# Values by slots, and position terms with keys on the partitions, turned by an identity product

## The chip, the cores and the metric

The kernel runs on one core of a Trainium2 chip. Its time is the device time of one execution in microseconds (us); the number to predict is the median of the runs. TensorE is called PE here, ScalarE ACT, VectorE DVE, GpSimd POOL, and SP is the engine that issues nearly all DMAs.

## What is computed

A decoder layer in float32 on x of 4 x 256 x 128 and a context of 4 x 512 x 128: local attention, cross attention, and a mixture of 12 experts. The change touches the first part alone:

```python
q_blocked = pad(q).reshape(B, nb, 12, 8, 16)          # 22 blocks of 12 queries, 8 heads of 16
k_ctx = _extract_block_context(k, nb)                 # 24 keys for each block: 12 past, 12 own
v_ctx = _extract_block_context(v, nb)
matrix_ac = einsum('bnchd,bnkhd->bhnck', q_blocked, k_ctx)
rel_k = (position_embeddings @ Wrel.T).reshape(-1, H, D)      # 25 positions
matrix_bd = _rel_shift(einsum('bnchd,phd->bhncp', q_blocked, rel_k))
logits = tanh((matrix_ac + matrix_bd) / 50) * 50
out = einsum('bhnck,bnkhd->bnchd', softmax(logits), v_ctx)
```

`_rel_shift` gives row c (query c of its block) the position term of key j at position j - c, with a wrap by one row: where j < c, the term is that of query c-1 at position j - c + 25.

## The kernel before, in words

Each engine has one program, written out by hand in the order in which it runs; semaphores join them. The 88 windows (4 batches x 22 blocks) are taken four at a time, 32 PSUM partitions each: 22 groups, in 6 chunks `c` of at most 4 groups. `qM` holds the queries of a window in 24 columns (12 for each half of the heads), `kM` the keys times a mask of four heads (`G` = 4), so that one product of 96 columns gives a window's logits for 24 keys and 4 heads. `relM` is the same for the 25 positions (100 columns).

PE, after the projections (`L863`): `relative(c)` multiplies every window's queries with `relM`; ACT copies the results to `bd_raw` (`positions_out`, `L631`), SP stores them in DRAM (`store_positions`, `L382`) and reads them back with rows one element further on each time (`shift_positions`, `L392`) into `bd`: that is the shift. `local_logits(c)` (`L922`) makes the key terms in PSUM, DVE adds `bd` (`add_positions`, `L1383`), ACT does tanh and exp in place (`local_softmax`, `L673`, `L675`), PE turns the result (`turn_weights_local`, `L931`), ACT copies it to `prT` (`weights_turned`, `L682`), and PE multiplies with the values (`local_values`, `L953`). DVE divides (`local_normalize`, `L1405`, `L1407`), PE turns (`turn_outputs`, `L966`) and projects (`local_project`, `L975`).

The values of a window must lie with 96 partitions = 24 keys x 4 heads in `vbd`, zero outside their own head. They go PSUM, `v_tok` (ACT `L638`), DRAM (`v_dram`, `L399`), `vbd` (24 DMAs, `spread_values`, `L351`, behind all the position traffic on SP).

Between the logits and the turned weights stand eight products of the cross attention, `unit(0)` to `unit(7)` (`L892`): four key units, each read by DVE (`key_unit`, `L1357`, `L1362`) with POOL adding the halves (`L506`), and four value units, read by ACT (`value_unit`, `L665`). They share two PSUM banks in turn, so that each waits for the reader of the one before the last. `local_values(0)` uses these banks as well. DVE's order after the key units: the first three `add_positions`, the statistics of contexts 1 to 3 (`L1294`), three more `add_positions`, their normalisation (`L1300`), then `local_normalize(0)`.

Of the kernel before, what the change touches and what calls it, by code (L numbers as in the profile page):

```python
# [7 lines left out]
P = 128  # L8
BANK = 512
F32 = mybir.dt.float32  # L10
F32R = mybir.dt.float32r
ALU = mybir.AluOpType
# [11 lines left out]
def decoder_layer(nc, x, ctx_in, pos, a_wq, a_wk, a_wv, a_wpost, a_wrel, a_pds,  # L24
# [31 lines left out]
    REL = NPOS * G  # L56
    SPREADS = 3
# [42 lines left out]
    with ExitStack() as ctx:  # L100
# [6 lines left out]
        bd_dram = nc.dram_tensor("bd_dram", [WALL, QW, REL], F32, kind="Internal").ap()  # L107
        gate_dram = nc.dram_tensor("gate_dram", [2, NE, 4 * P], F32, kind="Internal").ap()
        v_dram = nc.dram_tensor("v_dram", [B * SPAD, VROW], F32, kind="Internal").ap()
        psum = ctx.enter_context(nc.psum_tensor("psum", [P, 8, BANK], F32))  # L110

        REL_BANK = [3, 1, 7, 6, 0, 2]
# [16 lines left out]

        def half_groups(half):  # L130

            return slice(CG * HCH * half, min(CG * HCH * (half + 1), NGRP))
# [5 lines left out]
        def bank(i, parts=P):  # L138
# [45 lines left out]
        v_tok = sb("v_tok", [P, NT, HA, DE], F32, first)  # L184
        v_pad = sb("v_pad", [PAST, HA, DE], F32, first)
# [7 lines left out]
        relM = sb("relM", [P, NPOS, G], F32, first)  # L193
        vbd = sb("vbd", [GK, NW, G, 2, DE], F32, first)
        projected = ExitStack()
        xT = sb("xT", [P, B, S], F32, projected)

        bd_raw = sb("bd_raw", [P, NGRP, REL], F32, projected)
# [5 lines left out]
        first.close()  # L204

# [56 lines left out]
            ld_affine ld_wo ld_bo bd_stored0 bd_stored1 shifted0 shifted1 stored consts chain_pool chain_dve chain_act stats_done mv_done  # L262
            rstd_done xn_done absneg_done softplus_done qscale_done awT_ps awT_done xT_ps xT_done v_tok_ps v_tok_done pad_set v_zeroed v_padded v_stored v_spread0 v_spread1 v_spread2
            rel_ps relM_done q_ps k_ps qM_done kM_done bd_ps bd_raw_done added_done pT_ps pT_done logit_ps
# [72 lines left out]
        def _(sp):  # L337
# [7 lines left out]
            def spread_values(third):  # L345

                ns = spread_slots(third)
                windows = v_dram.rearrange("(n t) c -> t n c", t=CH)
                for g in range(G):
                    for part in range(2):  # L350
                        sp.dma_start(vbd[part * CH * G + g:(part + 1) * CH * G:G, ns, g, :, :].rearrange("t n h d -> t n (h d)"),  # L351
                                     windows[:, ns.start + part:ns.stop + part, g * 2 * DE:(g + 1) * 2 * DE]).then_inc(s[f"v_spread{third}"], 16)
# [13 lines left out]
            sp.wait_ge(s["pad_set"], 2)  # L366
            rows = v_dram.rearrange("(b r) c -> r b c", b=B)
# [1319 lines left out]
```

## Time and profile before

| | us |
|---|---|
| median of 3 runs | 478.07 |
| lowest, highest | 477.93, 480.35 |
| the profiled execution, whole | 479.27 |
| its span (first to last instruction) | 477.5 |
| PE busy, share of the span | 92% |
| DVE, POOL, ACT busy | 69%, 51%, 40% |

The rows come from the one profiled execution. A row of the chain of waits is a piece of the path that ended last; a row of the timeline is one or several instructions of an engine with their first start and their length. float32 products are two instructions each, so a row with x16 holds 8 products. PE's granted clock is 1.00 at 2.4 GHz and 0.50 at 1.2 GHz.

### The profile page before, as it was taken

What the parts mean: (1) busy time and instruction counts of PE and PEld (TensorE: products, weight loads), DVE (VectorE), ACT (ScalarE), POOL (GpSimd) and SP (SyncE); (2) the same over time, 40 slices, a digit from 0 to 9 for tenths busy, and PEclk for the clock granted to TensorE, in tenths of its full rate; (3) what the DMA queues carried; (4) which work ended last, traced back from release to release, by engine and by line L of the source; (5) the groups of instructions that cost most, each with busy time, mean ns of one, the idle gap of its engine ahead of it and who ended that gap; (6) DMA issues with size and microseconds to landing.
All of it is one profiled execution on the core that took longest, in us unless ns stands there. A gap on an engine that the chain in (4) does not pass through costs nothing.

```text
span 477.5 us, 8551 instructions
## 1 busy us (share of the span) xinstructions
PE 441.5 (92%) x3264; PEld 325.0 (68%) x3264; DVE 327.2 (69%) x688; ACT 188.7 (40%) x296; POOL 245.4 (51%) x217
## 2 busy tenths in 40 slices
PE   4977899999999999989999998779999999999996
PEld 2654676766666766657766675367777688888885
DVE  8886578979998577895779767635463543274544
ACT  7738046456445354553444543213344532300000
POOL 5783139896898768877677766114232333000000
PEclk9997799999999999999999999588999999999999
DMA  7754400000000000000000030230325140000000
GB/s 182 185 126 66 79 14 2 0 1 1 0 1 2 1 1 1 0 1 2 1 1 2 1 93 0 80 121 28 128 68 198 67 155 1 1 12 5 12 5 11
DMA packets 32810, 19.83 MB, mean 42 GB/s; under 512 B 16438, under 2 KB 29675, under 8 KB 32771
## 3 DMA queue, kind: packets, MB, share of 16 engines
q1 hardware_dynamic: 32068, 19.02, 14.6%
q8 instruction: 26, 0.43, 0.4%
q10 hardware_dynamic: 702, 0.28, 0.2%
q14 instruction: 14, 0.11, 0.1%
HBM read 17.27 MB, written 2.02 MB: 40 GB/s over the span
## 4 chain that ended last, share of the span: by engine, by line
PE 75%; DVE 14%; ACT 5%; issue 4%; POOL 2%; DVEq 0%; POOLq 0%; ACTq 0%
PE psum L1083 11%; PE psum L1066 9%; PE psum L892 9%; PE psum L1257 5%; PE psum L1256 5%; PE psum L1258 5%; PE psum L1220 4%; PE psum L1222 4%; PE psum L1221 4%; PE psum L1102 3%; PE psum L1093 3%; PE psum L995 2%; PE psum L1119 2%; DVE kM L1369 2%; PE psum L953 2%
## 5 line engine op out<-in xcount | busy, mean ns | idle before, releaser
L514 POOL TENSOR_TENSOR e_part<-e_sb 128x512 f32<-128x512 f32 x64 | 88.6, 1401 | 30.7 <-DVE e_sb L1467 30.7
L744 ACT ACTIVATE e_sb<-psum 128x1024 f32<-128x1024 f32 x64 | 62.2, 1022 | 17.0 <-PE psum L1066 16.8
L1083 PE MATMUL psum<-e_sb,v_sb 128*64 128x256 f32 x512 | 64.3, 394 | 0.0
L1066 PE MATMUL psum<-q_t,kT 64*128 64x256 f32 x512 | 64.3, 389 | 0.0
L545 POOL TENSOR_TENSOR xeT_lo<-xeT,xeT_hi 128x512 fp32r<-128x512 f32 x24 | 30.9, 1288 | 58.9 <-ACT xeT_hi L758 50.0
L1467 DVE TENSOR_SCALAR e_sb<-e_sb 128x1024 f32<-128x1024 f32 x64 | 56.2, 913 | 5.4 <-ACT e_sb L744 5.4
L1474 DVE RECIPROCAL rden<-psum 128x256 f32<-128x256 f32 x32 | 55.9, 1746 | 3.7 <-PE psum L1093 3.6
L1651 DVE SCALAR_TENSOR_TENSOR x_sb<-psum,dw,x_sb 128x128 f32<-128x128 f32 x96 | 33.6, 350 | 34.8 <-PE psum L1258 32.2
L1066 PEld LDWEIGHTS psum<-q_t,kT 64*128 64x128 f32 x512 | 47.0, 186 | 10.3 <-issue 5.4
L724 ACT ACTIVATE kT<-psum 128x512 f32<-128x512 f32 x32 | 19.1, 598 | 86.4 <-PE psum L995 86.4
L506 POOL TENSOR_TENSOR k_rot<-rope_a,rope_b 128x512 f32<-128x512 f32 x32 | 42.2, 1321 | 18.7 <-DVE rope_b L1362 18.7
L1083 PEld LDWEIGHTS psum<-e_sb,v_sb 128*64 128x64 f32 x512 | 34.4, 139 | 22.4 <-issue 6.9
L1220 PE MATMUL psum<-xeT_hi,w1T_hi 128*128 128x512 f32 x96 | 41.1, 428 | 3.4 <-POOL xeT_lo L545 3.4
L520 POOL TENSOR_TENSOR e_part<-e_part 128x512 f32<-128x512 f32 x32 | 41.5, 1296 | 2.5
L1221 PE MATMUL psum<-xeT_lo,w1T_hi 128*128 128x512 f32 x96 | 38.7, 403 | 0.0
L1222 PE MATMUL psum<-xeT_hi,w1T_lo 128*128 128x512 f32 x96 | 38.7, 403 | 0.0
L758 ACT ACTIVATE xeT_hi<-xeT 128x512 fp32r<-128x512 f32 x24 | 15.1, 632 | 58.9 <-DVE xeT L1506 36.1
L1256 PE MATMUL psum<-w2T_hi,h_hi 128*128 128x512 f32 x96 | 37.3, 389 | 0.0
L1257 PE MATMUL psum<-w2T_lo,h_hi 128*128 128x512 f32 x96 | 37.3, 389 | 0.0
L1258 PE MATMUL psum<-w2T_hi,h_lo 128*128 128x512 f32 x96 | 37.3, 389 | 0.0
L892 PE MATMUL psum<-wkv_hi,ctx_hi 128*128 128x512 f32 x64 | 31.5, 492 | 5.7 <-DVE rope_b L1362 5.7
L1357 DVE TENSOR_TENSOR rope_a<-psum,cos_sb 128x512 f32<-128x512 f32 x32 | 22.0, 686 | 20.3 <-PE psum L892 19.9
(191 smaller groups left out, 786.5 us busy)
## 6 DMA issues: line engine op xcount, KB each, us to landing
w_raw<-in_L_ffn_W_dram SPq DMA_DIRECT2D x24, 256.0 KB, 2.8
gates<-gate_dram SPq DMA_DIRECT2D x6, 768.0 KB, 4.4
ctx_sb<-in_ctx_dram SPq DMA_DIRECT2D x4, 256.0 KB, 6.1
vbd<-v_dram SPq DMA_DIRECT2D x16, 52.6 KB
v_dram<-v_tok SPq DMA_DIRECT2D x4, 136.0 KB, 3.1
raw<-in_L_xattn_Wkv_dram SPq DMA_DIRECT2D x2, 256.0 KB, 4.9
k_rot<-in_L_xattn_Wkv_dram SPq DMA_DIRECT2D x2, 256.0 KB, 4.9
k_rot<-in_L_xattn_Wq_dram SPq DMA_DIRECT2D x2, 256.0 KB, 5.4
```

Source lines behind the costliest of these rows:

```text
L514: pool.tensor_tensor(e_part[:, p % 2, half, :, :], e_sb[:, i % ERING, :, 0, :], e_sb[:, i % ERING, :, 1, :], ALU.add)\
L744: act.activation(e_sb[:, i % ERING, :, :, :].rearrange("p a k t -> p (a k t)"), psum[:, a:a + 2, :].rearrange("p a b -> p (a b)"), ACT.Exp ...
L892: mm = pe.matmul(o, c, w_[:, wc:wc + GC], start=(part == 0), stop=(part == 2))
L1066: mm = pe.matmul(psum[:, 2 * (i % 2) + a, t * S:(t + 1) * S], kT[rows, p % 3, kt * P:(kt + 1) * P], q_t[rows, j % 2, p % 2, :], start=True ...
L1083: mm = pe.matmul(psum[DX * a:DX * a + DX, pv_bank(p), 0:S], v_sb[g % 2][:, kt, 2 * pp + a, :], e_sb[:, i % ERING, a, t, :], start=(kt == 0 ...
L1220: pe.matmul(bank(c), w1T_hi[:, e, c, :], hi, start=(e == 0), stop=False)
L1221: pe.matmul(bank(c), w1T_hi[:, e, c, :], lo, start=False, stop=False)
L1222: mm = pe.matmul(bank(c), w1T_lo[:, e, c, :], hi, start=False, stop=(e == NE - 1))
L1256: pe.matmul(o, hi, w_hi, start=(c == 0), stop=False)
L1257: pe.matmul(o, hi, w_lo, start=False, stop=False)
L1258: mm = pe.matmul(o, lo, w_hi, start=False, stop=(c == HC - 1))
L1467: dve.tensor_scalar(e, e, E_LO, E_HI, ALU.max, ALU.min).then_inc(s["clip_done"], 1)
```

## The change

**Values.** `v_tok` gets one row for each of 96 slots (a slot is 12 padded tokens; 23 for each batch, 92 in all). 12 products (one for each token of a slot, the slot's columns of `xT` at a stride of 12) take the place of 8. `xT` gets its zero padding in SBUF, so the padding rows in DRAM go. `v_dram` is ordered token, head group, slot, so that each of the 24 spreading DMAs moves 12 long pieces instead of 12 x 33 short ones; the 3 stores before them have 96 x 16 pieces of 136 bytes each.

**Position terms.** `relative(j)` now has the positions as stationary operand: for query c of all 88 windows, the 96 columns of `relM` that begin at c positions less give keys on the partitions and windows on the columns, and a second product with the columns 25 positions on adds the wrap. 46 products of 64 rows x 96, 88 columns each; the two halves of the heads lie on the two halves of the rows. ACT copies them to `rel_t` (6 copies, 96 x 352). `local_logits` adds them in PSUM by a second product for each window, `rel_t` times the identity, 88 in all. The DRAM tensor `bd_dram`, its 8 stores and 16 loads, the 6 additions on DVE and the clearing of `bd` on POOL are gone.

**Order.** PE makes the values first, then the positions, then logits and turned weights in alternation, and only then units 1 to 7. ACT does the softmax before the value units. DVE makes all of `kM` before it normalises context 0.

```diff
-            def positions_out(c):
-                act.wait_ge(s["bd_ps"], c + 1)
-                ks = groups(c)
-                act.activation(bd_raw[:, ks.start:ks.stop, :].rearrange("p k r -> p (k r)"), psum[:, REL_BANK[c], 0:len(ks) * REL], ACT.Copy)\
-                   .then_inc(s["bd_raw_done"], 1)
+            def positions_out(n):
+                j, h = divmod(n, 2)
+                act.wait_ge(s["rel_t_ps"], j + 1)
+                q = h * CH + CPB * j
+                act.activation(rel_t[:, 0:WALL * QW].rearrange("p (w q) -> p q w", q=QW)[:, q:q + CPB, :],
+                               psum[0:GK, REL_BANK[n], 0:CPB * WALL].rearrange("p (c w) -> p c w", c=CPB), ACT.Copy).then_inc(s["rel_t_done"], 1)
...
-                act.wait_ge(s["added_done"], c + 1)
+                act.wait_ge(s["logit_ps"], c + 1)
...
-                act.activation(at, at, ACT.Tanh, scale=1.0 / CAP).then_inc(s["capped_done"], 1)
+                act.activation(at, psum[:, LOGIT_BANK[c], 0:len(ks) * GK], ACT.Tanh, scale=1.0 / CAP).then_inc(s["capped_done"], 1)
...
             def weights_turned(c):
                 act.wait_ge(s["pT_ps"], c + 1)
                 if c == 0:
-                    act.wait_ge(s["bd_stored1"], 16 * WG)
+                    act.wait_ge(s["v_stored"], 16 * len(VBANK))
...
+            def relative(j):
+                if j == 0:
+                    pe.wait_ge(s["relM_done"], G)
+                    pe.wait_ge(s["rel_set"], 2)
+                    pe.wait_ge(s["qM_done"], 8)
+                else:
+                    pe.wait_ge(s["v_tok_done"], 1 if j == 1 else 3)
+                queries_at = qM[:, 0:WALL * QW].rearrange("p (w q) -> p q w", q=QW)
+                for cc in range(CPB):
+                    c = CPB * j + cc
+                    main = slice(REL_AT - G * c, REL_AT - G * c + GK)
+                    wrap = slice(REL_AT + REL - G * c, REL_AT + REL - G * c + GK)
+                    for part in range(2 if c else 1):
+                        for h in range(2):
+                            rows = slice(64 * h, 64 * h + 64)
+                            mm = pe.matmul(psum[0:GK, REL_BANK[2 * j + h], cc * WALL:(cc + 1) * WALL], relM[rows, wrap if part else main],
+                                           queries_at[rows, h * CH + c - part, :], start=(part == 0), stop=(part == 1 or c == 0))
+                mm.then_inc(s["rel_t_ps"], 1)
...
+            def local_logits(c):
+                pe.wait_ge(s["kM_done"], G if c == 0 else 2 * G)
+                pe.wait_ge(s["rel_t_done"], len(REL_BANK))
...
+                        pe.matmul(psum[QT * i:QT * i + QT, LOGIT_BANK[c], at:at + GK], qM[:, QW * w:QW * w + QT],
+                                  kM[:, b, CH * n:CH * n + CTX, :].rearrange("p t g -> p (t g)"), start=True, stop=False)
+                    for i in range(WG):
+                        w = WG * k + i
+                        mm = pe.matmul(psum[QT * i:QT * i + QT, LOGIT_BANK[c], at:at + GK], rel_t[:, QW * w:QW * w + QT],
+                                       ident[0:GK, 0:GK], start=False, stop=True)
...
-            for c in range(HCH):
-                relative(c)
             values = awT[:, 2, :].rearrange("p (h g d) -> p g h d", h=2, g=G)
-            for t in range(NT):
...
+            for t in range(CH):
+                j, at = divmod(t, VT)
+                mm = pe.matmul(psum[0:SLOTS, VBANK[j], at * D:(at + 1) * D].rearrange("p (g h d) -> p g h d", g=G, h=2),
+                               xT[:, t:SLOTS * CH:CH], values, start=True, stop=True)
...
+            for j in range(CH // CPB):
+                relative(j)
             for c in range(NCH):
                 local_logits(c)
-            for m in range(UNITS):
+                if c == 1:
+                    turn_context(0, 6, "ct_ps")
+                if c >= 2:
+                    turn_weights_local(c - 2)
+            turn_weights_local(NCH - 2)
+            unit(0)
+            turn_weights_local(NCH - 1)
+            for m in range(1, UNITS):
                 unit(m)
-            for c in range(NCH):
-                turn_weights_local(c)
```

PE from the projections on, before: products by line, output<-operands, shape and count.

```order
L863 MATMUL psum<-xT,awT 128x512 x4
L908 MATMUL psum<-relM,qM 32x100 x48
L1018 MATMUL psum<-awT,xT 128x128 x8
L908 MATMUL psum<-relM,qM 32x100 x40
L870 MATMUL psum<-ident,ctx_sb 128x128 x4
L922 MATMUL psum<-kM,qM 32x96 x88
```

The same place after the change (`L1003` are the values, `L888` the positions, `L907` the identity products; the last two rows repeat to the end of each chunk).

```order
L839 MATMUL psum<-xT,awT 128x512 x4
L1003 MATMUL psum<-awT,xT 96x128 x12
L888 MATMUL psum<-qM,relM 96x88 x46
L903 MATMUL psum<-kM,qM 32x96 x4
L907 MATMUL psum<-ident,rel_t 32x96 x4
```

What moved: the 88 position products of 32 rows became 46 of 96 rows behind the values, and every four key products are followed by four identity products.

ACT from the position copies to the first copy of turned weights, before.

```order
L631 ACTIVATE bd_raw<-psum 128x400 x2
L631 ACTIVATE bd_raw<-psum 128x200
L647 ACTIVATE ctx_f<-psum,affine 128x512
L653 ACTIVATE ctx_hi<-ctx_f 128x512
L595 ACTIVATE wkv_hi<-k_rot 128x512 x2
L597 ACTIVATE wq_hi<-k_rot 128x512 x2
L691 ACT_TABLE_LOAD
L665 ACTIVATE v_sb<-psum 128x512 x4
L673 ACTIVATE bd<-bd 128x384
L675 ACTIVATE bd<-bd 128x384
```

The same stretch after the change.

```order
L612 ACTIVATE v_tok<-psum 96x32x16 x3
L607 ACTIVATE rel_t<-psum 96x4x88 x6
L569 ACTIVATE wkv_hi<-k_rot 128x512 x2
L571 ACTIVATE wq_hi<-k_rot 128x512 x2
L665 ACT_TABLE_LOAD
L645 ACTIVATE bd<-psum 128x384
L647 ACTIVATE bd<-bd 128x384
L621 ACTIVATE ctx_f<-psum,affine 128x512
L627 ACTIVATE ctx_hi<-ctx_f 128x512
L645 ACTIVATE bd<-psum 128x384
```

What moved: the context's copies (`L647`, `L653` before) went behind the first softmax, and the four value units (`L665` before) behind all of it.

## Rows read from the trace of the kernel before

**Rows 1.** Page, part 2: granted clock of PE in 40 slices of the span.

```profile
PEclk9997799999999999999999999588999999999999
```

**Rows 2.** The chain that ended last, in order of time: start us, length us, what.

```profile
25.39 3.18 PE psum L922 x144
28.57 0.91 PE psum L892 x3
...
37.71 0.60 ACT v_sb L665
...
46.43 3.80 PE psum L953 x128
50.24 1.03 PE psum L966 x4
...
52.44 0.60 PE psum L966 x4
...
58.51 1.99 PE psum L953 x64
...
79.54 1.93 PE psum L1066 x16
```

**Rows 3.** Timeline of PE: start, length, line, shapes [idle before].

```profile
16.07 2.27 PE L908 MATMUL psum<-relM,qM 128*32 128x100 f32 x96
18.27 2.05 PE L1018 MATMUL psum<-awT,xT 128*128 128x128 f32 x16
...
39.33 0.64 PE L931 MATMUL psum<-ident,bd 128*96 128x128 f32 x4 [1.65 <-ACT bd L675]
...
51.19 1.25 PE L953 MATMUL psum<-vbd,prT 96*32 96x68 f32 x64
```

**Rows 4.** Timeline of ACT.

```profile
17.03 0.51 ACT L631 ACTIVATE bd_raw<-psum 128x400 f32<-128x400 f32 x1
...
22.86 0.78 ACT L647 ACTIVATE ctx_f<-psum,affine 128x512 f32<-128x512 f32 x1 [0.22 <-PE psum L870]
...
24.21 1.13 ACT L595 ACTIVATE wkv_hi<-k_rot 128x512 fp32r<-128x512 f32 x2
...
26.40 1.28 ACT L691 ACT_TABLE_LOAD   x1
...
40.63 0.51 ACT L673 ACTIVATE bd<-bd 128x384 f32<-128x384 f32 x1
...
42.08 0.51 ACT L673 ACTIVATE bd<-bd 128x384 f32<-128x384 f32 x1
```

**Rows 5.** Timeline of DVE.

```profile
14.46 4.18 DVE L1369 TENSOR_SCALAR kM<-psum,mask 128x512 f32<-128x512 f32 x4 [1.97 <-PE psum L863]
...
29.57 0.69 DVE L1357 TENSOR_TENSOR rope_a<-psum,cos_sb 128x512 f32<-128x512 f32 x1 [1.62 <-PE psum L892]
...
34.92 1.48 DVE L1383 TENSOR_TENSOR bd<-psum,bd 128x384 f32<-128x384 f32 x3
36.32 0.86 DVE L1294 BATCH_NORM_STATS2 stats<-ctx_sb 128x6 f32<-128x128 f32 x4
...
41.02 3.15 DVE L1300 TENSOR_SCALAR ctx_sb<-ctx_sb,mv,rstd 128x128 f32<-128x128 f32 x12
48.52 0.36 DVE L1405 RECIPROCAL rq<-psum 128x32 f32<-128x32 f32 x1 [4.35 <-PE psum L953]
48.91 0.69 DVE L1407 TENSOR_TENSOR o_q<-psum,rq 128x512 f32<-128x512 f32 x1
```

**Rows 6.** Timeline of SP: issue of DMAs.

```profile
35.26 20.52 SPq L351 DMA_DIRECT2D vbd<-v_dram  x24
```

**Rows 7.** Page, DMA to landing of the values' stores: KB each, us to landing.

```profile
v_dram<-v_tok SPq DMA_DIRECT2D x4, 136.0 KB, 3.1
```

**Rows 8.** Stretches of 2 us: PE, PEld, DVE, ACT, POOL busy, PE's granted clock, DMA share, GB/s.

```profile
38.00:40.00 2.00, 0.64 (x4) 0.39 (x4) 1.93 (x15) 1.94 (x5) 1.92 (x3) 1.00 0.52 77
...
46.00:48.00 2.00, 2.00 (x62) 1.64 (x65) 0.00 (x0) 0.74 (x2) 0.00 (x0) 0.50 0.55 82
```

More of the change, by code:

```diff
@@ L56, in decoder_layer @@
     REL = NPOS * G
+    SLOTS = 96
+    CPB = 4
+    REL_AT = CH * G
+    VBANK = [0, 2, 3]
+    VT = CH // len(VBANK)
     SPREADS = 3
@@ L192, in decoder_layer @@
         pds = sb("pds", [P, 4], F32, first)
-        relM = sb("relM", [P, NPOS, G], F32, first)
-        vbd = sb("vbd", [GK, NW, G, 2, DE], F32, first)
+        relM = sb("relM", [P, REL_AT + REL + GK], F32, first)
+        vbd = sb("vbd", [GK, G, NW, 2, DE], F32, first)
         projected = ExitStack()
-        xT = sb("xT", [P, B, S], F32, projected)
-        bd_raw = sb("bd_raw", [P, NGRP, REL], F32, projected)
+        xT = sb("xT", [P, SLOTS * CH], F32, projected)
+        v_tok = sb("v_tok", [SLOTS, CH, G, 2, DE], F32, projected)
+        rel_t = sb("rel_t", [GK, WALL * QW + QT - QW], F32, projected)
         projected.close()
@@ L204, in decoder_layer @@
         first.close()
+        xT_b = xT[:, 0:B * SPAD].rearrange("p (b t) -> p b t", b=B)
+        vbd_all = vbd[:, :, :, :, :].rearrange("p g n h e -> p (g n h e)")
+        VZ = [G * NW * 2 * DE * i // 3 for i in range(4)]
         second = ExitStack()
@@ L526, in _ @@
                 key_sum(k)
[L527 to L528 removed]
+            pool.wait_ge(s["logit_ps"], NCH)
+            pool.wait_ge(s["v_stored"], 16 * len(VBANK))
             pitch = CG * P + CH
@@ L691, in _ @@
             act.preload_act_table(ACT.Exp)
-            for m in range(KC, UNITS):
-                value_unit(m)
             local_softmax(0)
+            act.wait_ge(s["ct_ps"], 1)
+            context_f(0)
             for c in range(1, NCH):
@@ L698, in _ @@
             weights_turned(NCH - 1)
+            for m in range(KC, UNITS):
+                value_unit(m)
             for c in range(HCH):
@@ L953, in local_values @@
                             mm = pe.matmul(psum[QT * i:QT * i + QT, o, at:at + G * DE].rearrange("p (g e) -> p g e", e=DE),
-                                           prT[:, q:q + QT], vbd[:, NBP * b + n, :, half, :], start=True, stop=True)
+                                           prT[:, q:q + QT], vbd[:, :, NBP * b + n, half, :], start=True, stop=True)
                 mm.then_inc(s["oa_ps"], 1)
@@ L1376, in _ @@
             dve.wait_ge(s["sin_done"], 1)
-            def add_positions(c):
-                dve.wait_ge(s["logit_ps"], c + 1)
-                dve.wait_ge(s[f"shifted{c // HCH}"], 16 * 2 * WG)
-                ks = groups(c)
-                dve.tensor_tensor(bd[:, ks.start:ks.stop, :].rearrange("p k r -> p (k r)"), psum[:, LOGIT_BANK[c], 0:len(ks) * GK],
-                                  bd[:, ks.start:ks.stop, :].rearrange("p k r -> p (k r)"), ALU.add).then_inc(s["added_done"], 1)
             for m in range(KC):
                 key_unit(m)
-            for c in range(HCH):
-                add_positions(c)
             for b in range(1, B):
                 context_statistics(b)
-            for c in range(HCH, NCH):
-                add_positions(c)
             for b in range(1, B):
```

137 lines of the change are left out of this document (43 added, 94 removed).

## The prediction

> **What bounds the kernel now.** I read the 40 slices first: PE's clock is full except in slices 4 and 5 (36 to 60 us) and around 300 us [rows 1]. The change acts before 66 us; from there on the chain is PE work in an unchanged order, so what counts is by how much its entry into that part moves. Next the chain of waits up to there. It goes through the last logits and the eight units (28.57 us on), then ACT's softmax after the last value unit (37.71), then the value products at 46.43, the first turned outputs at 50.24 and the second at 52.44 [rows 2]. The long idle piece is PE between 37.7 and 46.4: it waits for ACT, is busy 0.64 of 2 us, and enters the value products at 1.2 GHz [rows 8]. The position terms' trip through DRAM is not what ends last there: ACT is busy with value units until 38.3 us in any case. The spreading of the values is issued from 35.26 to 55.78 us [rows 6]; its last third is used at 58.51 [rows 2].
>
> **What the change does to each stage.** I follow four times: the end of the position products R, the end of the last copy to rel_t E, the start of unit 0 U, and the start of the second turned outputs T, which was 52.44 us [rows 2].
>
> *Values.* They start where the position products did, 16.07 us. Eight products took 2.05 us, 0.256 us each [rows 3]; twelve take 3.07 us and end at 19.14. The queries are complete at 17.03 [rows 4], so they don't bind.
>
> *Positions.* 46 products, 92 instructions of 64 rows with 96 stationary and 88 moving columns: no row has this shape. The 64-row products of the scores, whose halves lie on the two halves of the rows as here, take 1.93 us for 16 instructions with 256 moving columns [rows 2], 121 ns each; by moving columns 88/256 of that is 41 ns, by stationary columns (128 there) 96/128 of it is 90 ns. So 3.8 to 8.3 us. Before, 96 instructions of 32 columns took 2.27 us, but four of them lie side by side [rows 3]. I take the middle, 65 ns: the shape lies between the two scalings, since a narrow moving operand leaves less to hide the loading of weights behind. 6.0 us, so R = 25.1.
>
> The Trainium skill ("TensorE: Matmul & The Clock Gate", LDWEIGHTS) has the load of weights grow with its columns, at 1.2 per ns, and lets it run ahead of a product only where the row groups differ. By that 96 columns are 80 ns, 7.4 us in all if loads never lie side by side, and the result would be 481.3; no row here shows a load of 96 columns in a stream.
>
> *Copies to rel_t.* 400 columns took 0.505 us [rows 4]; 352 take about 0.46 if the spread writing costs nothing. DVE's kM copy, which writes one float32 of four, takes 1.05 us for 512 columns where its rope_a product takes 0.69 [rows 5], a factor of 1.5. So 0.46 to 0.70; I take 0.55. Four of the six hide beside the products; the last two follow R: E = 25.1 + 0.15 + 1.1 = 26.4 us.
>
> *ACT from E to U.* The four weight copies (24.21 to 26.40) and the table load of 1.28 us come behind the copies: 3.5 us [rows 4]. Then a softmax of 0.97 (tanh 0.51 and exp of the same length, overlapped), the context's two copies that moved here, 1.35 (22.86 to 24.21), three rounds of softmax and copy at 1.45 (40.63 to 42.08) and a last softmax of 0.97 [rows 4]: 7.65. PE then turns once more, 0.64 [rows 3], so U = E + 11.8. PE's own work in the same time is less: 176 logit products are 352 instructions at 22 ns (144 in 3.18 us [rows 2]), 7.8 us, twice before; five turns at 0.6 and the context's turn make 11.4. It is hidden by 0.4 us only; if the switch between key and identity products costs 30 ns instead of 22, PE is later by 2.4 us. U = 38.2 us. DVE's six additions (three in 1.48 us [rows 5]) go, but what they held up stood behind the value units anyway.
>
> *Units and values.* The eight units still alternate over two banks with DVE: 28.57 to 38.3 with the last copy, 9.8 us [rows 2]. So value products start at U + 9.85 = 48.0, where before it was 46.43. That is the cost of the change: the softmax, which stood behind the units, now stands ahead of them, and what PE gains by not waiting it spends on logits. They then run at 2.4 GHz: 128 instructions take 2.5 (64 in 1.25 [rows 3]) where they took 3.80 [rows 2]. PE is through both at 50.5.
>
> *What is late next: DVE.* Its order keeps context statistics and normalisation between the key units and the first division. The key units end 6.4 us after U (28.57 to 34.92, where the additions began). From the first statistics to the normalisation went 4.7 (36.32 to 41.02), of which the second three additions, one of half size, were 1.2 by the 1.48 of the first three; so statistics take 3.5, normalisation 3.1 [rows 5], which before ended at 44.2 with room to 48.52. Now it ends at U + 13.1 = 51.3, and the division takes 1.08 (48.52 to 49.60 [rows 5]): turned outputs start at 52.4, not 50.24. So half of the gain of the full clock goes into a wait for DVE. Then turn 0.6, values 1.2: T = U + 16.0 = 54.2 against 52.44, +1.8 us. From there the chain is the one of before.
>
> *DMA.* Three stores of 1536 pieces each take the place of four of 256. The nearest issue row is the spreading, 24 issues of up to 396 pieces in 20.52 us [rows 6], 2.2 ns a piece: 3.3 us each. They start at about 17.8, end by 27.7 and land 3.1 later [rows 7], 30.8. ACT's first turned copy needs them at E + 6.8 = 33.2. Between a price by bytes alone (0.5 us each) and this, nothing waits. The 24 spreading DMAs with 12 pieces end long before 48 us at any of these prices; their old cost was hidden, so nothing is gained.
>
> *The rest at nothing.* The clearing of bd, the padding's memsets and the small relM memsets on POOL lie ahead of work that waits for statistics. Where that cover is gone, they cost under 0.5 us.
>
> **The sum.** +1.8 us at the entry into the unchanged part. The profiled execution took 479.27, its span 477.5, the rest 1.8 around it; it lies 1.2 above the median of 478.07. By its own measure it would be 481.1, by the median **479.9 us**.
>
> **The rivals.**
> *A, the halves pair fully.* 92 instructions at 43 ns, 4.0 us, copies of 0.46: R = 23.1, E = 24.2, U = 36.0, T = 52.0, -0.4: 477.6. For it: the scores' halves do pair. Against it: there the moving part is three times as long. Chance 0.25.
>
> *B, strided reading.* The queries are read with 96 bytes between columns, the slots' weights with 48. If every column costs a second access, the halves' gain is lost: 88 ns each, 8.1 us, copies 0.70: R = 27.2, E = 28.8, U = 40.6, T + 4.2: 482.3. For it: DVE's kM row [rows 5]; against it: no PE row shows such a cost. Chance 0.15. The Trainium skill ("SBUF — State Buffer", the note on cachelines) states this: lines of 16 bytes, and at least two hits in each for full bandwidth.
>
> *C, the stores hold ACT.* The first turned copy now waits for v_stored. It decides from a store of 4.1 us on; at 5.8 each they land at 38.3, ACT stands 5.1 us, and all behind it: 485.0. For it: 136-byte pieces, 4608 of them; against it: the issue row gives 3.3. Chance 0.07.
>
> *D, the clock.* The dip in which 64 instructions take 1.99 and not 1.25 us (58.51 us [rows 2, 3]) goes, since PE no longer stands idle ahead of it: -1.3 beside A's -0.4: 476.4, and a little below with the later dip near 300 us moved. Against it: the work just ahead of 58 us is as thin as before, and there is a new gap of 1.9 us before the turned outputs. Chance 0.08.
>
> **Chances.** Forecast 0.45 (478.5 to 481.8), A 0.25, B 0.15, C 0.07, D 0.08. About 0.5%, 2.4 us, is what a measurement can tell from no change. Below 475.7 lies the end of D, 0.05; above 480.5 lie B, C and two fifths of the forecast, 0.40; within, 0.55. The range takes in A, B and most of D, with 2 us for B's upper bounds (the identity products at 30 ns): 476.2 to 484.0.
>
> **What would show it.** Position products of 6 us ending near 25; ACT's first tanh near 30; unit 0 near 38 and value products near 48 at clock 1.00; then DVE normalising contexts while PE stands until about 52.4. It would be wrong if DVE had done its contexts earlier (the gain of the clock is then real, -1.5), if the identity products run slower than 22 ns, or if PE's clock falls between 25 and 48 us.

## The result, and the profile after

The changed kernel takes 490.78 us (median of 4 runs, 489.21 to 493.47), the kernel before 478.00 in the same session: a ratio of 1.027, 95% interval 1.020 to 1.033. It is slower, and 10.9 us above the 479.9 that was predicted, outside the range. The profiled execution took 489.21, its span 487.5 against 477.5. It is the fastest of its four, and the profiled execution of before lies above its median, so the profiles show 10.0 of the 12.8 us between the medians. Some executions further below ran slower at a lower granted clock, among them the profiled one of `y_layout` (0.85 on the mean), whose rows are therefore not shown, and all ratios leave them out.

The slices first, then the timeline of PE after the change (start, length, line, shapes, idle before).

```profile
PEclk9959989999999999999999999787999999999999
```

```profile
15.94 4.90 PE L1003 MATMUL psum<-awT,xT 128*96 128x128 f32 x24
20.77 10.33 PE L888 MATMUL psum<-qM,relM 64*96 64x88 f32 x92
...
33.16 0.55 PE L903 MATMUL psum<-kM,qM 128*32 128x96 f32 x8 [2.07 <-issue]
...
37.49 0.36 PE L903 MATMUL psum<-kM,qM 128*32 128x96 f32 x8
...
56.79 2.23 PE L938 MATMUL psum<-vbd,prT 96*32 96x68 f32 x128 [0.89 <-ACT v_sb L637]
61.04 0.97 PE L951 MATMUL psum<-ident,o_q 128*128 128x128 f32 x4 [2.02 <-DVE o_q L1384]
61.94 2.06 PE L938 MATMUL psum<-vbd,prT 96*32 96x68 f32 x64
63.93 0.98 PE L951 MATMUL psum<-ident,o_q 128*128 128x128 f32 x4
...
70.12 1.25 PE L938 MATMUL psum<-vbd,prT 96*32 96x68 f32 x64
```

The second turned outputs begin at 63.93 us; before they began at 52.44 [rows 2]. So 11.5 us are lost ahead of the part that the change leaves alone, 1.5 are given back behind it (0.7 of them by the value products at 70.12, which take 1.25 us where those of before at 58.51 took 1.99 [rows 2]), and 10.0 remain in the span. The loss is all in the first rows. The 92 position instructions take 10.33 us, 112 ns each, and the 24 of the values 4.90, 204 ns each. After them the logits wait 2.07 us. The row names no releaser, but the code lets the first logit product go when all six position copies are done, and the last of them ends at 33.06 us, 0.10 before it. The copies are these (timeline of ACT):

```profile
24.10 1.92 ACT L607 ACTIVATE rel_t<-psum 96x352 f32<-96x352 f32 x2 [2.63 <-PE psum L888]
...
31.14 1.92 ACT L607 ACTIVATE rel_t<-psum 96x352 f32<-96x352 f32 x2 [1.60 <-PE psum L888]
```

Two copies take 1.92 us. By itself a copy takes 1.10 us; one of as many elements takes 0.46 in `x_copies` below, so it is not their number that costs. The third thing to see is the clock, in stretches (PE, PEld, DVE, ACT, POOL busy, PE's granted clock, DMA share, GB/s):

```profile
20.00:22.00 2.00, 2.00 (x17) 1.79 (x18) 2.00 (x3) 0.59 (x1) 0.00 (x0) 1.00 1.11 122
22.00:24.00 2.00, 2.00 (x22) 1.83 (x20) 1.49 (x5) 0.00 (x0) 0.00 (x0) 0.92 1.65 64
24.00:26.00 2.00, 2.00 (x22) 2.00 (x20) 0.00 (x0) 1.90 (x2) 0.00 (x0) 0.50 1.45 61
```

PE is shown as busy for the whole of every stretch, and yet its granted clock falls from 1.00 (2.4 GHz) to 0.50 (1.2 GHz) in the middle of the position products. The products themselves do not notice: 22 records in a stretch at 0.92 as at 0.50. What comes behind does: a group of eight logit instructions starts 0.32 us after the last while the clock is low, and 0.17 us after it from 37.5 us on.

Of DMA, the store's landing (page) and the issues and waits of SP:

```profile
v_dram<-v_tok SPq DMA_DIRECT2D x3, 204.0 KB, 7.4
```

```profile
18.34 3.47 SPq L375 DMA_DIRECT2D v_dram<-v_tok  x3
29.33 19.28 SPq L351 DMA_DIRECT2D vbd<-v_dram  x24
```

```profile
SPq L351 <- DMA v_dram<-v_tok: 7.4, 1, 7.4
...
SPq L375 <- ACT v_tok L612: 2.5, 2, 1.3
```

### The profile page after: what moved, and what is told of

It reads as the page before. It is cut to its first block, busy times and chain, and to the rows that moved or that the text cites. A ratio compares the mean times of both kernels' runs of the same rounds, so it can differ in the third digit from the quotient of the medians.

```text
span 487.5 us, 8718 instructions
## 1 busy us (share of the span) xinstructions
PE 451.2 (93%) x3364; PEld 336.1 (69%) x3364; DVE 321.0 (66%) x682; ACT 192.3 (39%) x297; POOL 243.5 (50%) x220
## 4 chain that ended last, share of the span: by engine, by line
PE 76%; DVE 12%; issue 4%; POOL 4%; ACT 3%; DVEq 0%; POOLq 0%; ACTq 0%
PE psum L1072 11%; PE psum L1055 9%; PE psum L868 8%; PE psum L1247 4%; PE psum L1246 4%; PE psum L1245 4%; PE psum L1209 4%; PE psum L1211 4%; PE psum L1210 4%; PE psum L1091 3%; PE psum L1082 2%; PE psum L980 2%; PE psum L888 2%; PE psum L1108 2%; DVE x_sb L1416 1%
## 5 line engine op out<-in xcount | busy, mean ns | idle before, releaser
L488 POOL TENSOR_TENSOR e_part<-e_sb 128x512 f32<-128x512 f32 x64 | 88.6, 1400 | 30.8 <-DVE e_sb L1444 30.8
## 6 DMA issues: line engine op xcount, KB each, us to landing
vbd<-v_dram SPq DMA_DIRECT2D x16, 52.6 KB
```

The costliest lines, as they stand in the source:

```text
L488: pool.tensor_tensor(e_part[:, p % 2, half, :, :], e_sb[:, i % ERING, :, 0, :], e_sb[:, i % ERING, :, 1, :], ALU.add)\
```

## The experiments

Theory P: the shape of the products is cheap, and what costs is the place of their operands. The 88 moving columns of a position product stand 24 float32 apart in `qM`, the 96 stationary columns of a value product 12 apart in `xT`, and the position copies write every 24th float32 of `rel_t`. The rival S (the expectations below call it H, and give the letter S to the stride): the shape itself costs (96 columns of stationary operand for 88 of moving), or the halves of the rows do not run side by side.

### One operand at a time

`x_queries`, the position products read neighbours (the numbers are then other queries):

```
-                                           queries_at[rows, h * CH + c - part, :], ...
+                                           qM[rows, (h * CH + c - part) * WALL:(h * CH + c - part + 1) * WALL], ...
```

> The position products read 88 neighbouring columns of the queries instead of one column in 24 (so they multiply the wrong queries; all else stays). Theory S, the stride of the moving operand is the price: the 92 instructions, 10.3 us in the changed kernel at 111 ns each, fall to 4 to 6 us (43 to 65 ns), PE's clock stays at 1.00 behind them, so the first logits go at 22 ns an instruction instead of 40, and the kernel is 6 to 8 us faster than the changed one, 482 to 484 us. Theory H, the two halves of 64 rows don't run side by side, or the loading of 96 stationary columns is the price: still 8 to 10 us, and 490 us.

```profile
21.15 4.14 PE L888 MATMUL psum<-qM,relM 64*96 64x88 f32 x92
```

```profile
22.62 5.43 ACT L607 ACTIVATE rel_t<-psum 96x352 f32<-96x352 f32 x6 [0.77 <-PE psum L888]
```

486.88 us (one run). 45 ns an instruction in place of 112: S falls, the shape with its halves side by side costs about what rival A of the prediction had said (43). The six copies now stand in a row on ScalarE, one every 0.90 us, and PE waits for them from 25.3 to 28.1; behind that wait its clock falls instead (PE alone; busy, clock, DMA share, GB/s):

```profile
24.00:28.00 4.00, 1.29 (x32) 0.98 1.04 47
28.00:32.00 4.00, 3.86 (x116) 0.59 0.07 18
```

The second turned outputs begin at 58.54, 5.4 us earlier than in the changed kernel.

`x_slots`, the value products take neighbouring tokens:

```
-                               xT[:, t:SLOTS * CH:CH], values, start=True, stop=True)
+                               xT[:, t * SLOTS:(t + 1) * SLOTS], values, start=True, stop=True)
```

> The value products load 96 neighbouring columns of xT as stationary operand instead of one in 12 (values of the wrong tokens). Theory S for stationary operands: 24 instructions take 3.1 us instead of 4.9 (128 ns instead of 204), all behind is 1.8 us sooner, 488 us. Rival: 96 of 128 columns, or the change of shape, costs this; 4.9 us stay and 490 us.

```profile
16.00 2.78 PE L1003 MATMUL psum<-awT,xT 128*96 128x128 f32 x24
```

486.17 us (one run). 2.78 in place of 4.90 us, 116 ns each; the positions behind them stay at 10.32. The second turned outputs begin at 60.16, later than in `x_queries`, and yet the whole is no longer: here PE's clock is 1.00 from 36 us to 68, and 64 value products take 1.25 us, where in `x_queries` they take 2.06 (0.50 from 56 to 68). A single run of such a kernel can't be read to better than that.

`x_copies`, the copies write neighbours:

```
-               act.activation(rel_t[:, 0:WALL * QW].rearrange("p (w q) -> p q w", q=QW)[:, q:q + CPB, :],
+               act.activation(rel_t[:, q * WALL:(q + CPB) * WALL].rearrange("p (c w) -> p c w", c=CPB),
```

> ACT's six copies write 352 neighbouring columns of rel_t instead of one in 24 (so the logits get the position terms of other windows). Theory S for writes: a copy takes 0.46 us instead of 1.10, the last two end 1.0 to 1.2 us sooner behind the position products, and the kernel is 1 to 2 us faster, 488 to 489 us. Rival: the length comes from reading PSUM; the copies stay at 1.1 us and nothing moves.

```profile
32.42 0.81 ACT L607 ACTIVATE rel_t<-psum 96x352 f32<-96x352 f32 x2 [2.71 <-PE psum L888]
```

492.12 us (one run): a pair takes 0.81 us in place of 1.92 (one copy 0.46 in place of 1.10), and there is no gain in the time. Its position products began 1.3 us later than in the changed kernel, because the projections ahead of the values took 5.96 us and not 4.69; this stretch, which the edit does not touch, takes 4.69 to 6.35 us from trace to trace. And its value products at 71.55 ran at the low clock (2.06 us). What the stride of the copies costs is 1.1 us, on the pair at the end.

`x_three`, all three edits at once:

> All three together: neighbouring columns in the position products, in their copies and in the value products. Theory S: 1.8 + 5 + 1.1 us on PE and ACT ahead of the logits and about 2 us by the clock behind them, so unit 0 starts at 37 to 38 us instead of 46.9, and the kernel takes 479 to 481 us, as the prediction on record had it. Theory H: no better than 486 us.

```profile
16.91 2.78 PE L1003 MATMUL psum<-awT,xT 128*96 128x128 f32 x24
19.62 4.14 PE L888 MATMUL psum<-qM,relM 64*96 64x88 f32 x92
24.73 0.37 PE L903 MATMUL psum<-kM,qM 128*32 128x96 f32 x8 [0.96 <-issue]
...
47.30 2.22 PE L938 MATMUL psum<-vbd,prT 96*32 96x68 f32 x128 [0.89 <-ACT v_sb L637]
51.56 0.66 PE L951 MATMUL psum<-ident,o_q 128*128 128x128 f32 x4 [2.03 <-DVE o_q L1384]
...
53.58 1.12 PE L951 MATMUL psum<-ident,o_q 128*128 128x128 f32 x4
```

480.61 us, ratio 1.006 (1.003 to 1.009) to before. Three changes of address, with as many instructions on as many elements, take away 10.2 of the 12.8 us. P holds. The clock shows 1.00 from 20 to 52 us, so its fall in the changed kernel goes with the operands too.

### Do the halves run side by side?

`x_halves` (strided) and `x_q_halves` (neighbours) issue all products of the upper half of the rows, then all of the lower, instead of taking turns:

```
-                for cc in range(CPB):
...
-                        for h in range(2):
+                for h in range(2):
+                    for cc in range(CPB):
```

> The changed kernel with the position products of one half of the heads all ahead of those of the other (same 46 products, same strides, other order in each of the three parts). If the two halves of the rows run side by side, this takes it away. Theory S (the stride holds the stream at about 111 ns an instruction whatever the clock): with side by side lost, each instruction waits for its own stream, 150 to 220 ns, 14 to 20 us for the 92. Theory H (they never ran side by side): 10.3 us stay.

> The same order by halves with neighbouring columns of the queries (wrong queries are multiplied). x_queries took 4.14 us for the 92 instructions, 45 ns each. If the halves run side by side there, this gives about 80 ns each, 7.0 to 8.0 us; if not, 4.1 us stay.

```profile
21.11 16.40 PE L888 MATMUL psum<-qM,relM 64*96 64x88 f32 x92
```

```profile
22.20 6.72 PE L888 MATMUL psum<-qM,relM 64*96 64x88 f32 x92
```

Strided 178 ns an instruction, neighbours 73; taking turns 112 and 45. So alternation saves 37 to 38% in either case, and the stride costs a factor of 2.4 to 2.5 in either case: two effects that multiply. The times were 496.36 and 488.16 us (one run each). The Trainium skill ("TensorE: Matmul & The Clock Gate", LDWEIGHTS) has a load take its columns over 1.2 in ns, an estimate of 80 ns for 96 columns, and the same page lets a load run beside a product only where their row groups differ. The traces agree in kind: issued by halves an instruction takes 73 ns, and taking turns 45. The estimate is too high here, since 73 ns hold a load and its product.

### How far apart is far?

`x_strides` reads the moving columns of the three groups of position products at every 2nd, 4th and 12th float32, the stationary columns of the three groups of values at every 2nd, 4th and 8th.

```
+                                           qM[rows, 0:WALL * (2, 4, 12)[j]:(2, 4, 12)[j]], ...
+                               xT[:, 0:SLOTS * (2, 4, 8)[j]:(2, 4, 8)[j]], values, ...
```

> The kernel after with other strides, and so with other numbers in its output: the position products take their moving operand at every 2nd, 4th and 12th column of the queries in their three groups, and the value products their stationary operand at every 2nd, 4th and 8th column in theirs. The two ends are known: 111 ns per position instruction at every 24th column and 45 ns side by side; 204 ns per value instruction at every 12th column and 116 ns side by side. Theory G (the price grows with the distance of neighbours until each stands in a stretch of memory of its own): groups of positions at 45 to 65, 65 to 111 and 111 ns, groups of values near 116 to 140, 140 to 204 and 204 ns. Rival N (anything but neighbours side by side pays the whole): 111 ns in all three groups and 204 ns in all three. Rival B (only a great distance costs): 45 ns at 2 and 4 and 111 ns at 12. The time as a whole is not argued from this run.

```profile
21.00 6.45 PE L888 MATMUL psum<-qM,relM 64*96 64x88 f32 x92
```

```profile
19.67 0.60 ACT L612 ACTIVATE v_tok<-psum 96x512 f32<-96x512 f32 x1 [0.81 <-PE psum L1003]
21.11 0.59 ACT L612 ACTIVATE v_tok<-psum 96x512 f32<-96x512 f32 x1 [0.84 <-PE psum L1003]
22.48 1.92 ACT L607 ACTIVATE rel_t<-psum 96x352 f32<-96x352 f32 x2 [0.77 <-PE psum L888]
25.01 1.92 ACT L607 ACTIVATE rel_t<-psum 96x352 f32<-96x352 f32 x2 [0.61 <-PE psum L888]
27.50 1.92 ACT L607 ACTIVATE rel_t<-psum 96x352 f32<-96x352 f32 x2 [0.58 <-PE psum L888]
```

ACT's copies mark the ends of the groups. Moving operand: the first copy starts 1.48 us after the first product, as with neighbours in `x_three` (21.09 after 19.62), so 8 bytes between columns cost nothing. The second and third groups, 32 instructions each, take 2.53 and 2.49 us from copy to copy, 79 and 78 ns at 16 and 48 bytes; by the same measure 96 bytes cost 110 (3.52 us between the copies of the changed kernel) and neighbours 43 (1.37 us). Stationary operand: 1.44 us for eight instructions at 32 bytes, 180 ns, and 1.41 at most at 16 bytes, 176 ns; by the same measure 48 bytes cost 202 and neighbours 109. The eight at 8 bytes can't be told apart from neighbours: the first two groups together take 2.4 us.

None of the three theories is quite it. There is a step between 8 and 16 bytes, a flat piece up to 48, and for the moving operand a second step up to 96. This second step rests on two kernels: `x_strides` reads the same columns again in every product of a group, the changed kernel others in each, and no run has 96 bytes with the same columns. So it is likely, and not shown, that the distance alone makes the second step; the same holds for 180 ns at 32 bytes and 202 at 48. The Trainium skill ("SBUF — State Buffer", the note on cachelines) states the first: lines of 16 bytes, and two accesses to each for full bandwidth. The rows agree: with two columns to a line nothing is lost, and one to a line costs 36 ns on 43. 488.59 us (one run), from which nothing is argued.

### The order of the stages, and DVE

The prediction held the new order (softmax ahead of the units) for the cost of the change. `t_units_first` is `x_three` with the units and their copies ahead of the softmax again, `t_contexts` is `x_three` with DVE's statistics and normalisation of the later contexts ahead of the units.

```
+            turn_context(0, 6, "ct_ps")
             for c in range(NCH):
                 local_logits(c)
...
+            for m in range(UNITS):
+                unit(m)
+            for c in range(NCH):
+                turn_weights_local(c)
```

> x_three (no strides, so some of its data are wrong) with the order of the kernel before: the context turned ahead of the logits, all eight units on PE and the value copies on ACT ahead of the softmax, the turned weights last. Theory O, the order is what costs in x_three: PE stands for ACT's softmax behind the units as before, clock falls, value products start 1 us sooner or later than in x_three, but DVE's context work lies beside the softmax, so the second turned outputs start near 51 us instead of 53.6; 477 to 479 us. Rival: the order is worth nothing, 480 to 481 us.

```profile
54.65 3.61 PE L938 MATMUL psum<-vbd,prT 96*32 96x68 f32 x128
...
59.97 0.66 PE L951 MATMUL psum<-ident,o_q 128*128 128x128 f32 x4
```

485.26 us, ratio 1.016 (1.013 to 1.019): 4.7 us worse than `x_three`. PE waits for the softmax, enters the value products at the low clock (128 in 3.61 us) and turns the second outputs at 59.97 in place of 53.58. So the new order is not the cost; in this kernel, with twice as many logit instructions as before, going back on it costs more than 4 us. Not all of that is the wait for the softmax, though. In the logits, which now come in one piece, PE stops three times with no releaser:

```profile
28.07 0.27 PE L907 MATMUL psum<-ident,rel_t 96*32 96x96 f32 x2 [0.78 <-issue]
...
32.49 0.28 PE L907 MATMUL psum<-ident,rel_t 96*32 96x96 f32 x2 [1.55 <-issue]
...
36.03 0.28 PE L907 MATMUL psum<-ident,rel_t 96*32 96x96 f32 x3 [0.67 <-issue]
```

Counted from the first value product, the second outputs come 5.7 us later than in `x_three`. These stops are 3.0 us, in `x_three` 0.38 in the same stretch, so they make 2.6 of the 5.7; what they are is read further below.

```
             context_normalize(0)
+            for b in range(1, B):
+                context_statistics(b)
+            for b in range(1, B):
+                context_normalize(b)
             context_lo(0)
```

> x_three with DVE's statistics and normalisation of contexts 1 to 3 (and POOL's part of them) moved ahead of the key units, where DVE stands idle. The prediction's step: DVE then holds nothing behind the key units, the first turned outputs start at about 50 us instead of 51.6 (2.0 us of idle PE go), PE's clock stays up, and the kernel is 2 to 3.5 us faster than x_three: 477.5 to 478.5 us. Rival: POOL or DVE are late for the first unit and the gain is lost; 480.5 us.

```profile
50.40 0.66 PE L953 MATMUL psum<-ident,o_q 128*128 128x128 f32 x4 [0.20 <-DVE o_q L1386]
50.99 1.04 PE L940 MATMUL psum<-vbd,prT 96*32 96x68 f32 x50
54.01 0.47 PE L940 MATMUL psum<-vbd,prT 96*32 96x68 f32 x14 [1.98 <-issue]
```

480.17 us, and 479.1 over the eight runs that the ratio of 1.002 (0.998 to 1.005) counts: between the theory and its rival, and not clear of `x_three` (1.003 to 1.009). The wait for DVE shrinks from 2.03 to 0.20 us, as expected, but PE then stops for 1.98 us in the middle of a run of products, with nothing that releases it, and in this execution the gain is gone at once (second outputs at 54.41). It took 481.30 us, the longest of those eight; the shortest took 475.48. Whether all of them have the stop no trace says.

### The layout put right

`y_layout` leaves nothing out. ScalarE writes the queries a second time, by position in the chunk, into the space of `bd`; the values are taken 96 neighbouring tokens at a time and go through DRAM by token; the position copies write runs of four.

```
+            qc = qC.rearrange("p (c b n) -> p b c n", b=B, n=NB)
+                act.activation(qc[:, bs, :, 0:full], ps[:, :, 0:full * CH].rearrange("p b (n c) -> p b c n", c=CH),
+                               ACT.Copy, scale=pds[:, 3:4]).then_inc(s["qC_done"], 1)
...
+                                           qC[rows, (c - part) * WALL:(c - part + 1) * WALL], ...
...
+                               xT[:, t * SLOTS:(t + 1) * SLOTS], values, start=True, stop=True)
...
+                act.activation(rel_t[:, 0:WALL * QW].rearrange("p (w q) -> p w q", q=QW)[:, :, q:q + CPB],
+                               psum[0:GK, REL_BANK[n], 0:CPB * WALL].rearrange("p (c w) -> p w c", c=CPB), ACT.Copy)
```

> The change with its data laid out side by side, nothing left out: ScalarE writes the queries a second time by position in the chunk, from the same PSUM, so that the position products read 88 neighbours; the value products take 96 neighbouring tokens, with the DRAM copy of the values by token and read back in pieces of 136 bytes; the copies of the turned terms write runs of four and read PSUM at every 88th element. Theory P (the loss is the place of the operands alone): values 2.8 us, positions 4.1 to 4.3 us, copies 0.8 to 1.4 us per two, positions begin 0 to 1 us later than in the kernel with all three laid out wrongly, because ScalarE writes the second queries first; second turned outputs at 53.6 to 55.5, 480.5 to 482.5 us. Rival W (runs of four are no better than single elements): copies 1.9 us per two, the last logits wait for ScalarE, second turned outputs at 57 to 59, 485 to 487 us. Rival D (the many small pieces of the read back come late): a wait for the spread values ahead of the value products, 484 us or more.

479.42 us, ratio 1.003 (1.000 to 1.006) to before: 11.4 us better than the changed kernel, and 1 us under what P had said. The rows are read from `y_full` below, which holds the same edits.

`y_split` lets DVE copy two of the six turned terms and normalises and turns the first context earlier.

```
+                    if j == 1 and g in (1, 2):
+                        dve.wait_ge(s["rel_t_ps"], g + 1)
+                        dve.tensor_copy(rel_t[:, 0:WALL * QW].rearrange("p (w q) -> p w q", q=QW)[:, :, q:q + CPB], ...
...
+            turn_context(0, 6, "ct_ps")
             for c in range(NCH):
                 local_logits(c)
-                if c == 1:
-                    turn_context(0, 6, "ct_ps")
```

> The kernel with the laid-out data, and besides: VectorE copies two of the six turned terms, between its masked keys; the first context is normalised between the two halves of the keys, and turned ahead of the first logits, into the idle time of TensorE there. Theory P: the last turned term is in place 0.5 to 1 us after the last position product, TensorE is idle under 0.5 us there, the units end 0.5 to 1.2 us earlier than with the laid-out data alone; 479.3 to 481 us, and within 0.5% of the kernel before. Rival V (VectorE is late): its second copy waits behind the masked keys and the logits start later than with ScalarE alone, 481 us or more. Rival F (faster than before): the products out of DRAM's way start 1.5 us earlier than in the kernel before and 476 to 477.5 us follow; I give this 0.1, since TensorE's own work is 2.6 us more than before.

```profile
50.60 0.99 PE L951 MATMUL psum<-vbd,prT 96*32 96x68 f32 x49
52.78 0.70 PE L951 MATMUL psum<-vbd,prT 96*32 96x68 f32 x15 [1.19 <-issue]
```

480.76 us, ratio 1.004 (1.000 to 1.007). Unit 0 starts at 35.71 in place of 37.27 in `x_three`, and again a stop without a releaser, 1.19 us, eats it: the second outputs turn at 53.42, against 53.58.

`y_full` is `y_split` with the early contexts of `t_contexts`, and loads the 512 KB of output weights only after the last outputs are turned.

```
+            sp.wait_ge(s["oT_done"], NCH)
             sp.dma_start(wo_sb[:, :, :], x_wo.rearrange("(c p) n -> p c n", p=P)).then_inc(s["ld_wo"], 16)
```

> The kernel with the laid-out data, two turned terms copied by VectorE and the context turned early, and on it two moves: the statistics and normalisation of the other three contexts stand on VectorE behind its last masked keys, ahead of the units; the load of the 512 KB of output weights waits until the last outputs are turned. In the trace without these moves TensorE stops 2.0 us for VectorE's first normalised outputs and 1.2 us in the middle of the third value products with no releaser, a stop that ends as the 512 KB land; with the contexts early alone there was a stop of 2.0 us at the same place. Theory L (the stop is TensorE's own instructions, which come by DMA, late behind the 512 KB): no stop without a releaser between 45 and 60 us; second turned outputs at 50 to 51.5 us, 476 to 478.5 us. Rival I (the stop belongs to the place in the program): 1 to 2 us without a releaser remain in the third or fourth value products, second turned outputs at 52 to 53.5 us, 479 to 481 us. Rival C (the granted clock takes it back): no stop, but 0.50 of the clock over more of 50 to 66 us, 479 to 481 us.

```profile
17.55 2.78 PE L1019 MATMUL psum<-awT,xT 128*96 128x128 f32 x24
...
37.52 0.47 PE L882 MATMUL psum<-wkv_hi,ctx_hi 128*128 128x512 f32 x1 [0.76 <-issue]
...
50.56 1.55 PE L954 MATMUL psum<-vbd,prT 96*32 96x68 f32 x64
52.05 0.66 PE L967 MATMUL psum<-ident,o_q 128*128 128x128 f32 x4
```

```profile
21.74 0.81 ACT L621 ACTIVATE rel_t<-psum 96x352 f32<-96x352 f32 x2 [0.77 <-PE psum L903]
```

```profile
29.46 7.35 DVE L1304 TENSOR_SCALAR ctx_sb<-ctx_sb,mv,rstd 128x128 f32<-128x128 f32 x12
36.73 0.68 DVE L1352 TENSOR_TENSOR ctx_lo<-ctx_f,ctx_hi 128x512 fp32r<-128x512 f32 x1
```

478.09 us, ratio 1.001 (0.999 to 1.003): as fast as before, not faster. The stop in the value products is gone, as L had it, but the second outputs came at 52.05, not at 50 to 51.5. The two DVE rows say why: the twelve normalisations of the contexts take 7.35 us here (7.37 in `t_contexts`; 3.31 behind the units, at 56.68 in the changed kernel; why they are slower here is open), the first unit needs the context's low part that stands behind them, and starts at 37.5 instead of 35.7. Two copies in runs of four, with PSUM read at every 88th element, take 0.81 us, as much as with neighbours on both sides. By `y_full` alone it is not settled whether the load had held PE up: two things were moved at once, and the landing of the load fits the end of the stop only in `y_split` (52.6 us and 52.8); in `t_contexts` it landed at 55.1, a microsecond after the stop had ended.

The traces say what the stops are. Among the DMA queues of the page is one named `instruction`, whose packets are 16 KB each (queue: packets, MB, share):

```profile
q8 instruction: 27, 0.44, 0.4%
```

Count the records of PE (loads of weights, products, semaphore events) from the start of the span. Every stop without a releaser inside a run of products then stands at one of four records: at 449 in `x_three` (0.38 us), `t_contexts` (1.03) and `t_units_first` (0.78), at 705 and 961 in `t_units_first`, at 1473 in `t_contexts` and `y_split`. All are 449 plus a multiple of 256. And each stop ends 1.3 to 2.2 us after the end of one packet of that queue: the first for record 449, the second for 705, the third for 961, the fifth for 1473. In none of the 14 traces does such a record begin less than 1.28 us after the end of its packet. That leaves little but L's account of the stops: PE waits for its own instructions. What makes a packet late is less certain. The fifth one starts 2.9 and 3.8 us after PE has reached record 1217 in `t_contexts` and `y_split`, whose 512 KB were in flight at that time, and 0.9 in `y_full`; elsewhere it is 0.4 to 1.5. That is for L's other half, the load, but in `x_queries` and `x_strides` the load was in flight too and the packet no later than 1.5 us. And the stops at 449, 705 and 961 come long before the load is issued.

## Why the prediction was wrong, point by point

From 52.44 the second turned outputs were to move to 54.2 and moved to 63.93, 9.7 us further. By its steps:

- **Values.** 3.07 us forecast, 4.90 measured; the positions began at 20.77, not 19.14: +1.6. The 0.256 us a product was taken from rows whose stationary operand lies side by side. With neighbours the twelve take 2.78 us, so the scaling was good and the stride was left out; rival B had named the stride for this very operand, and priced only the positions.
- **Positions.** This is the step that failed: 65 ns an instruction, 112 measured, 6.0 against 10.33 us, +4.3. The two parts of it were both wrong. The shape costs 45 ns, near rival A's 43, so the middle between the two scalings was too high; and the forecast put the stride of the queries at nothing, where it costs 67 ns on top. Rival B had the stride, but stopped at 88, because it took back only the gain of the halves. `x_halves` shows that the stride multiplies what the halves leave. Had B's sum been made from the one row with a factor in it (DVE's copies) it would still have been too low, since that factor was 1.5 and is 2.5 here. The kind of rival was right, its 0.15 too little, its price half.
- **Copies.** 0.55 us, bounds 0.46 to 0.70; 1.10 measured, and 0.46 without the stride. The last two end 1.96 us behind the positions, not 1.3: +0.7. The bound from DVE's row, which writes one float32 of four, did not hold for one of 24.
- **From the copies to unit 0.** 11.8 us forecast, 13.7 measured (33.06 to 46.75): +1.9. The clock accounts for the first part of it: in `x_three`, at 1.00 throughout, it is 12.6 (24.63 to 37.27). The remaining 0.8 is mostly PE's own work, which was held to be hidden by 0.4 us and is not: ACT waits for turned weights there (0.38 and 0.52 us in `x_three`), and PE's sum of 11.4 had nothing for the pauses before each of the six turns, nor for the stop of 0.38. That PE's clock might fall between 25 and 48 us stood among the things that would make the prediction wrong, and it had fallen by 24, in a stretch in which PE is shown busy throughout. No row of before had such a case: there the clock falls while PE waits.
- **From unit 0 on.** Value products at U + 9.85 forecast, U + 10.0 measured. DVE's last normalisations end at 59.91, U + 13.2 against U + 13.1, and the first outputs turn at U + 14.3 against 14.2, behind a wait of 2.02 us for DVE. That half of the clock's gain goes into a wait for DVE's contexts was right: `t_contexts` moves them, and the wait is 0.20 us. Then 64 value products took 2.06 and not 1.2 us, the clock having fallen in that wait: +1.2 with the turn.
- **The dip of rival D.** The later one did go (1.25 us at 70.12, 1.99 before), and a new one came ahead of it (2.06 at 61.94). D's gain was cancelled by a dip that it had not foreseen.
- **Order.** The forecast called the softmax ahead of the units the cost of the change. `t_units_first` says the reverse: without it the kernel is 4.7 us slower, in part by stops of PE that the forecast knew nothing of.
- **DMA.** Nothing waited for it, as forecast, but the prices were wrong. The three stores take 3.47 us with 2.5 of waits, about 0.3 us each, not 3.3; they land 7.4 us later, not 3.1. The two errors cancel: 29.3 against 30.8. The spreading takes 0.80 us an issue with 12 long pieces, 0.86 before with up to 396 [rows 6], and in `y_full`, with pieces of 136 bytes again, 0.86: the price of an issue is hardly by the piece.

The sum of the terms is 1.6 + 4.3 + 0.7 + 1.9 + 1.2 = 9.7. Against `x_three` the three strides are 2.1 + 6.2 + 1.1 = 9.4 us; its second outputs come 11.3 us earlier, counted from the first value product, so about 1.9 us belong to the clock that fell with them.

## What to carry to other kernels

Cost a product by its shape from a row and then ask, for each operand and each output by itself, how many bytes lie between neighbouring columns; here that factor was 2.5 on the moving operand, 1.8 on the stationary one and 2.4 on ScalarE's writes, and none of it shows in the list of instructions. Where a layout must be strided somewhere, put the stride where it costs nothing (here ScalarE's read of PSUM at every 88th element) and write short runs. A stage can lose the clock without standing still: after a long strided stream, read the granted clock and not the busy share. And where PE stops with no releaser, count its records up to the stop and look at the `instruction` queue before you look for a cause in the data.

## What the runs showed of the hardware

- A float32 moving operand of 88 columns, the halves of the rows taking turns, from copy to copy: 43 ns an instruction with neighbours and at 8 bytes, 79 at 16, 78 at 48, 110 at 96; the last was the same at a granted clock of 1.00 and 0.50.
- A stationary operand of 96 columns, by the same measure: 109 ns with neighbours, 180 at 32 bytes, 202 at 48. In both lines the figures between the first and the last are from products that read the same columns again each time, the last is from products that read others.
- ScalarE's copy of 96 x 352 float32 out of PSUM: 1.10 us with every 24th float32 written, 0.46 with neighbours or runs of four.
- The granted clock fell from 1.00 to 0.50 inside a stream with which PE is shown busy without a gap, in all runs with 112 or 178 ns an instruction (`x_copies` 0.78 in 24 to 28 us and 0.50 in 28 to 32; `x_slots` 0.98, then 0.50), and in none at 45 to 79 ns.
- PE stopped 0.4 to 2.0 us inside a run of products without a releaser in four kernels (`x_three`, `t_units_first`, `t_contexts`, `y_split`), seven times in all, always at record 449 of PE or a multiple of 256 behind it, and until 1.3 to 2.2 us after the end of a 16 KB packet of the `instruction` queue. What makes the packet late is open.
